# Two float32r score parts in 64-row tiles, in a two-layer transformer kernel

## The reference

```python
# layer 0: causal attention
qkv = x @ w_qkv
dots = einsum('bhid,bhjd->bhij', q, k) * d ** -0.5
dots = where(triu(ones, k=1), -inf, dots)
x = layernorm(x + (softmax(dots) @ v) @ w_out + b_out)
# ffn 0: ternary weights, silu(x @ wu) * (x @ wg) @ wd
# layer 1: 4 key/value heads shared by 16 query heads
q = (x * sigmoid(sum(abs(x)))) @ Wq;  k, v = split(x @ Wkv)
qk = q @ k.T / sqrt(16) - slope[h] * abs(i - j)
qk = where(abs(i - j) <= 32 or i < 64 or j < 64, -1e9, qk)
x = layernorm(x + (softmax(qk) @ v) @ Wo + bo)
# ffn 1: silu(x @ w_gate.T) * (x @ w_up.T) @ w_down.T
```

## Time and profile before

| what | us |
|---|---|
| median of 3 runs | 1196.45 (1194.09 to 1198.43) |
| the profiled execution | 1192.84 |
| its span, first to last instruction | 1191.1 |
| TensorE busy in the span | 1013.9 (85%) |
| VectorE busy | 734.6 (62%) |
| ScalarE busy | 576.1 (48%) |
| GpSimd busy | 323.0 (27%) |

### The profile page before, as it was taken

The page is one execution under the profiler, slowest core; times in us unless marked ns, Lnnn a source line. Parts: engine busy times, 40 slices in busy tenths (PEclk is TensorE's granted clock), DMA queues, the critical chain, the costliest instruction groups (busy, mean ns, idle before and its releaser), DMA issues. The chain is left out here.

```text
span 1191.1 us, 18123 instructions
## 1 busy us (share of the span) xinstructions
PE 1013.9 (85%) x6562; PEld 513.9 (43%) x6562; DVE 734.6 (62%) x1611; ACT 576.1 (48%) x1169; POOL 323.0 (27%) x391
## 2 busy tenths in 40 slices
PE   7924889989998899868468899999999998899996
PEld 4511232323333578654022333333333333588885
DVE  3653677777773556556457587777878773434422
ACT  3411466666665534316035476666767665423220
POOL 1040011111111345500433614224133240333332
PEclk9855899999999999969569799999999999999998
DMA  8585044333300000004952426254252100000001
GB/s 273 123 153 61 1 55 54 39 40 41 45 2 1 1 1 1 1 19 100 235 131 92 108 61 119 73 96 84 60 110 82 48 2 1 1 1 19 6 13 36
DMA packets 39636, 71.02 MB, mean 60 GB/s; under 512 B 7103, under 2 KB 23375, under 8 KB 38708
## 3 DMA queue, kind: packets, MB, share of 16 engines
q1 hardware_dynamic: 37660, 64.89, 26.8%
q0 software_dynamic: 1072, 3.80, 0.9%
q10 hardware_dynamic: 816, 1.18, 0.3%
HBM read 57.27 MB, written 12.32 MB: 58 GB/s over the span
## 5 line engine op out<-in xcount | busy, mean ns | idle before, releaser
L849 ACT ACTIVATE prob<-ps 128x512 f32<-128x512 f32 (+6 forms) x896 | 426.6, 539 | 341.3 <-PE ps L885 339.3
L885 PE MATMUL ps<-qop,kop 98*128 98x512 bf16 (+15 forms) x1376 | 285.3, 293 | 47.5 <-DMA qop<-mrow 29.0
L871 PE MATMUL ps<-kop,qop 96*128 96x512 bf16 (+4 forms) x896 | 265.3, 373 | 54.6 <-DVE maxes L790 27.9
L885 PEld LDWEIGHTS ps<-qop,kop 107*128 107x128 bf16 (+2 forms) x1376 | 108.2, 99 | 280.4 <-ACT prob L849 150.3
L912 PE MATMUL ps<-prob,vst 128*32 128x512 f32 (+4 forms) x1792 | 213.7, 549 | 5.2 <-POOL prob L739 5.2
L790 DVE CUSTOM_DVE_ANT_0 attn<-ps,alibi_table 128x960 bf16<-128x960 f32 x128 | 148.0, 1156 | 84.3 <-PE ps L871 67.8
L739 POOL TENSOR_TENSOR prob<-prob,keep 128x384 int32<-128x384 int32 (+2 forms) x144 | 121.2, 850 | 253.6 <-ACT prob L849 252.6
L790 DVE CUSTOM_DVE_ANT_0 tri<-ps,alibi_table 128x960 bf16<-128x960 f32 x128 | 147.8, 1155 | 24.1 <-PE ps L871 23.5
L1248 PE MATMUL ps<-xs,ffn_parts 128*128 128x512 f32 x640 | 150.5, 392 | 4.4 <-DVE hf L1222 2.3
L871 PEld LDWEIGHTS ps<-kop,qop 96*128 96x128 bf16 x896 | 77.7, 100 | 147.3 <-DVE maxes L790 82.7
L1248 PEld LDWEIGHTS ps<-xs,ffn_parts 128*128 128x128 f32 x640 | 119.0, 188 | 29.8 <-DVE hf L1222 3.1
(11 more groups left out here) (97 smaller groups left out, 722.2 us busy)
## 6 DMA issues: line engine op xcount, KB each, us to landing
alibi_table<-in_table SPq DMA_DIRECT2D x64, 336.0 KB, 4.3
qop<-q_parts SPq DMA_DIRECT2D x96, 128.0 KB, 7.1
kop<-k_parts SPq DMA_DIRECT2D x48, 128.0 KB, 7.8
kop<-k_parts SPq DMA_DIRECT2D x48, 96.0 KB
q_parts<-qop SPq DMA_DIRECT2D x8, 384.0 KB, 3.4
q_parts<-kop SPq DMA_DIRECT2D x8, 384.0 KB, 6.2
x<-in_x SPq DMA_DIRECT2D x4, 512.0 KB, 7.2
out<-x SPq DMA_DIRECT2D x4, 512.0 KB, 2.9
```

The costliest lines, as they stand in the source:

```text
L849: nc.scalar.activation(prob[0:rows, q % 2, k % HG, lo % CH:lo % CH + hi - lo], ps[0:rows, tile_bank(n, k), lo % CH:lo % CH + hi - lo], ACT ...
L871: last = nc.tensor.matmul(ps[:, slot + a // CH, a % CH:a % CH + b - a], qop[0:RD, par, qt // CT, h, i0 % CH:i0 % CH + P], kop[0:RD, par, h ...
L885: return nc.tensor.matmul(ps[0:rows, bank, a % CH:a % CH + b - a], lhs, rhs, start=start, stop=True, skip_group_check=True)
```

## The change

Scores are now made from two float32r parts (high: rounded to 12 bits of mantissa; low: the rest) in three products, high-high, high-low and low-high: 48 rows (`DOT`), with four position rows in layer 1 and two rows of maxima, 50 or 54 rows in all. Two heads of a pair stand in the two halves of the partitions, from row 0 and from row 64 (`ROW_TILE`), so that their matmuls address different 64-row tiles of the array. The units of a pair now alternate between the two heads. In `project` ScalarE writes the high part and VectorE the low one; the slots for parts are eight. The units of layer 0 come in another order, so that the parts of the first groups are ready first, and groups 0 and 1 are loaded within `project` in layer 0. The load of a group is 10 DMAs (12 in layer 1), some of 32 and some of 16 partitions, of float32. Layer 1 has two buffers (`L.bufs`) and loads group n + 1 at the third key tile of group n, held until the values of group n - 1 are done. The maxima are transposed in float32 and split after that. In `attend` the first rows of maxima are sent before the last group's load, and in layer 1 also before the second table. Position rows are rounded once at the start on GpSimd and written to DRAM. In layer 1 the last key tile of 64 keys is computed as a tile of 128, whose upper 64 lanes are used.

```diff
-RING = 4
+RING = 8
-PARTS = 3
-Q_PART = (0, 0, 0, 1, 1, 2)
-K_PART = (0, 1, 2, 0, 1, 0)
-BUFS = 3
+PARTS = 2
+HP = HG // 2
+ROW_TILE = P // 2
+DOT = 3 * HD
-NPOS = 9
+NPOS = 4
...
-        self.key_sets = HG if index == 0 else 3
+        self.key_sets = HP if index == 0 else 3
+        self.bufs = 3 if index == 0 else 2
...
-    return [(h, qt, *maximum_columns(layer, qt)) for half in range(2) for h in range(HG)
-            for qt in range(half * CT, (half + 1) * CT)]
+    return [(h, qt, *maximum_columns(layer, qt)) for half in range(2) for pair in range(HP)
+            for qt in range(half * CT, (half + 1) * CT) for h in (2 * pair, 2 * pair + 1)]
...
-            if q == 3 and BUFS <= n + 2 < N:
-                steps.append(("load", 0, n + 2))
+            if q == 3 - layer.index and n + layer.bufs - 1 < N:
+                steps.append(("load", 0, n + layer.bufs - 1))
...
+            for u in range(len(units)):
+                if u == first + 2:
+                    for k in range(first):
+                        sp.wait_ge(sent[k], stored(first, k))
                     operands.load(sp, 0)
+                elif u == first + 4 and L.bufs > 2:
+                    operands.load(sp, 1)
                 sp.wait_ge(part2, u + 1)
+                store(sp, u)
...
+                raw = K.staging
+                pool.dma_start(raw[0:QROWS, :], dram.qpos).then_inc(const_loaded, 16)
+                pool.dma_start(raw[QROWS:QROWS + KROWS, 0:T], dram.kpos).then_inc(const_loaded, 16)
...
+                nc.gpsimd.tensor_copy(rounded[0:QROWS, :], raw[0:QROWS, :]).then_inc(ones_set, 1)
...
-            def second_part(u):
-                r = rows_of(units[u][1])
-                act.wait_ge(rest1, u + 1)
-                nc.scalar.copy(part[u % RING][0:r, 1, :], rest[0:r, u % RING, :]).then_inc(part2, 1)
...
-            def third_part(u):
...
                 nc.vector.scalar_tensor_tensor(
-                    out=rest[0:r, u % RING, :], in0=ps[0:r, 2 + u % 4, :], scalar=0.25 if is_q(m) else 1.0,
-                    in1=part[u % RING][0:r, 0, :], op0=ALU.mult, op1=ALU.subtract).then_inc(rest1, 1)
+                    out=part[u % RING][0:r, 1, :], in0=ps[0:r, 2 + u % 4, :], scalar=0.25 if is_q(m) else 1.0,
+                    in1=part[u % RING][0:r, 0, :].bitcast(F32), op0=ALU.mult, op1=ALU.subtract).then_inc(part2, 1)
...
+        for a in range(2):
+            at = a * ROW_TILE
...
+            sp.dma_start(kop[at:at + 2 * HD, buf], key).then_inc(self.loaded[buf], 16)
+            sp.dma_start(kop[at + 2 * HD:at + DOT, buf], key[0:HD]).then_inc(self.loaded[buf], 16)
+            for e in range(2):
+                sp.dma_start(qop[at:at + 2 * HD, buf, e].rearrange("p h t -> p (h t)"),
+                             q_parts[0:1, e, n, a].to_broadcast((2, HD, HP * CH))).then_inc(self.loaded[buf], 16)
+            sp.dma_start(qop[at + 2 * HD:at + DOT, buf].rearrange("p e h t -> p e (h t)"),
+                         q_parts[1, :, n, a].rearrange("e d x -> d e x")).then_inc(self.loaded[buf], 16)
...
             if i == 1:
                 load_tables(0)
-                load_tables(1)
-            operands.load(sp, 1)
-            for k in range(RING):
-                sp.wait_ge(operands.sent[k], K.parts_in_dram[k])
-            operands.constants(sp, BUFS - 1)
-            operands.load(sp, BUFS - 1)
             for what, k, n in steps:
                 if what == "rows":
                     send_rows(n, k)
+                    if n == 0 and k == 0:
+                        if i == 1:
+                            load_tables(1)
+                        for slot in range(RING):
+                            sp.wait_ge(operands.sent[slot], K.parts_in_dram[slot])
+                        operands.constants(sp, L.bufs - 1)
+                        operands.load(sp, L.bufs - 1)
...
-                        nc.vector.tensor_copy(mrow[:, k, :], ps[:, ring_bank(what, k, n), :].bitcast(BF16)[:, 0:P]).then_inc(m_copied, 1)
+                        nc.vector.tensor_copy(mrow[:, k, 0, :], turned).then_inc(m_high, 1)
+                        dve.wait_ge(m_high, r + 1)
+                        nc.vector.tensor_tensor(mrow[:, k, 1, :], turned, mrow[:, k, 0, :].bitcast(F32),
+                                                ALU.subtract).then_inc(m_copied, 1)
...
-                i0 = qt * P
+                i0, at = qt * P, h % 2 * ROW_TILE
...
-                                            qop[0:RD, par, qt // CT, h, i0 % CH:i0 % CH + P],
-                                            kop[0:RD, par, h if i == 0 else 0, a:b], start=True, stop=True)
+                                            qop[at:at + RD, par, qt // CT, h // 2, i0 % CH:i0 % CH + P],
+                                            kop[at:at + RD, par, h // 2 if i == 0 else 0, a:b], start=True, stop=True)
...
-                        pe.wait_ge(m_cut, 2 * n + k + 1)
-                        nc.tensor.transpose(ps[:, ring_bank(what, k, n), :].bitcast(BF16)[:, 0:P],
-                                            mpart[:].rearrange("p k u -> p (k u)"), identb[:]).then_inc(m_turned, 1)
+                        pe.wait_ge(max_done, (2 * n + k + 1) * (NU // 2))
+                        nc.tensor.transpose(ps[0:NM, ring_bank(what, k, n), 0:P],
+                                            maxes[:, k].rearrange("p h t -> p (h t)"), ident[:]).then_inc(m_turned, 1)
```

288 lines of the change are left out of this document (138 added, 150 removed).

## The result

The changed kernel takes 1449.15 us (median of 6 runs, 1436.36 to 1466.12) against 1196.21 of the kernel before: ratio 1.2104, 95% interval 1.2068 to 1.2141. I had forecast 1180, faster. Its profiled execution, the fastest of the six, spans 1434.6 us against 1191.1, 243.5 more.

What follows compares the result with a forecast made beforehand. Attention takes most of the span, and TensorE never rests inside layer 1's key tiles. Terms -9 - 15 - 9 - 2 + 5 + 5 + 8.5 = -16.5 from 1192.84 give 1176.3, with 3.6 for the median 1180; range 1165 to 1195.

Steps and rivals of the forecast that it cites:

- step 3: Steady groups of layer 0: heads side by side -1.9 a group, weights and shape changes +0.8; -9 us in all.
- step 6: Steady groups of layer 1: side by side, weights and shape changes +5 us in sum, late operand loads +8.5.
- Steps 1 and 2: Layer 0's start: eight slots end the projection's slot wait, -9 us; first rows of maxima wait less behind loads, -15.
- the stores kept the rows of maxima waiting over 8 us: Sign of being wrong in kind, at layer 0's first rows of maxima, whose wait was taken as 3 us.
- Steps 4 and 5: Layer 1's start: 4, rows land sooner but second table as late as now, -2 us; 5, group 0's mask late, +5.
- Step 6 b: Layer 1's steady groups: float32 weight loads set the pace of short pieces, +2.5 us a group, between 0 and 6.1.
- Step 6 a: Layer 1's steady groups: tiles and units in different array halves overlap, -2.3 us a group, ends 0 and 9.
- Step 6 d: Layer 1, two buffers: operand load 1.4 us late in each of 6 groups against a 13.8 us window, +8.5.
- four-pass pieces: Rival: short float32r pieces take four passes, heads side by side; +16 us, 1196, 16%. The slower rival assumes them too.
- The loads at 122 GB/s: Rival: layer 1's operand loads run at 122 GB/s, 6 x 2.9 = +17 us, 1197, no change; 14%.
- The slower rival: Rival: short pieces take four passes and nothing runs side by side, in both layers' groups; 1252 us, 18%.

Runs made afterwards that it cites:

- e7: On top of e5, each score and exp matmul contracts 112 to 118 rows instead of 48 to 54, buffers filled ahead; 1239.48 us.
- e11: e2 with layer 1's tables, constants and operands ahead of its first rows of maxima again, as in the kernel before; 1331.73 us, ratio 1.1210 to before.
- e8: Kernel before, bf16 parts in 96 rows, with only the change's start of layer 0; 1172.88 us, ratio 0.9836.
- e2: On top of e1, parts of k stored by one transfer a unit over 128 (64) DRAM rows and loaded 16 rows at a time; 1353.26 us.
- e3: Kernel before, with first rows of maxima of each layer sent before loads of later operands and second tables; 1205.32 us, ratio 1.0093.
- e5: On top of e2, all four heads read the operands of rows 0 to 53, so one row tile; 1601.89 us.
- e1: Changed kernel, with each load repeating 16 rows of q twice replaced by loads of 16 rows each; 1369.56 us in one run.
- e4: Kernel before, with its bf16 score matmuls contracting 48 rows instead of 96, nothing else changed; 1286.60 us in one run.

## Why the prediction was wrong

It failed in what it took for granted, more than in its terms: above all in step 3 and step 6, whose groups were priced at a granted clock that the changed kernel doesn't get.

- **Granted clock: not a term at all.** I worked every duration at the clock of the rows before, in the one sentence of step 6 that I needed it and in all the others unsaid. The matmuls keep their columns, so I took them to keep their time. Rows 1 show the clock at 0.96 to 0.98 with 96 to 107 rows and no more can be read from them; that contraction over 48 rows in one tile need not keep it was not considered, and no rival had it. Set at full clock by e7, the steady groups cost 10.3 + 35.4 = 46 us more than before; in e11, whose transfers are the best that I tried together, they cost 57.3 + 78.3 = 136. The 90 us between are mostly the clock; late operands of layer 1 are in them too (28.9 us of idle time in e11, 11.1 of it before the groups), and what two tiles give back is taken off them.
- **Steps 1 and 2 (-24): right, then undone.** The mechanism is shown by e8 (first "exp" matmul at 82.02, forecast 81; 22.3 us at the end of the first group) and by e2 (78.51). In the changed kernel the first "exp" matmul stands at 115.06 instead of 105.32, so the same steps ended at +9.7, and the first group, at a granted clock of 0.52 instead of 0.79, adds 12.8 to make the 22.5 of the table. They ended there because I counted the stores by their bytes ("512 KB per unit instead of 384") and not by their form. I listed "the stores kept the rows of maxima waiting over 8 us" as a sign against me. They did worse: they kept the projection's slots, 7.63 and 4.84 us, and the block's end.
- **Step 3 (-9): wrong sign.** The groups stand 40.8 us apart, not 32.3. Of that 7.4 us, 1.5 is float32r at full clock (e7), where I had +0.8 for weights and shapes, and side by side takes 1.2 off again, where I had 1.9. The terms of the step were of the right kind; the rest, 7 us a group, is the clock.
- **Steps 4 and 5 (+3): mis-sized.** The first rows sent early in layer 1 cost 16.9 us in bf16 (e3) and 20.4 in float32r (e2 to e11). There are two chains. Step 4 had the second tables as late as the 9.3 us of before; VectorE waited 14.40 us for them in e3 and 16.14 in the changed kernel, and 31.24 instead of 16.28 for the first one behind the slow stores. The other is that of step 5, weights to GpSimd to the mask to TensorE (9.68 us in e3, 17.85 in the changed kernel), for which I took 18.8 us of slack from the earlier trace rows and reckoned the queue at the rate of an empty one. What I took as a gain of 5.7 us, rows that land sooner, was there (TensorE waits 3.17 us for them instead of 7.74), and was worth less than the queue behind it.
- **Step 6 b (+2.5 a group): the mechanism right, the size near its upper end.** At full clock the group costs 5.1 more (e7), against ends of 0 and 6.1. The records of the weight loads, 209 ns and more, don't refute the 129 that I took as their pace, as those of the feed-forward stage are as long at that pace. A part of the 5.1 is one that I put at nothing: the earlier trace rows gave 0.235 us for a float32r matmul of 512 columns, and I worked the long pieces as if they kept the 0.21 of the full clock. At 15 ns each for the hundred or so matmuls of 416 columns and more in a group, that is 1.6 us, an estimate. (The upper end by the skill's figure is 4.5, not 4.6; nothing hangs on it.) What it does was not quite what I said: ScalarE gets the first "exp" tile 0.18 us later, and the key tile is 3.29 us long against 2.88; that the chain of banks carries the delay on is my reading of it.
- **Step 6 a (-2.3 a group): right, and hidden by the clock.** Matmuls of two heads do start together: in the steady stretch of e2, 68 of 364 score and "exp" matmuls start within 20 ns of the one before, and none in e5. At the full clock that gives some 2.4 to 3.4 us a group in layer 1 against e7. The 249 us from e5 to e2 are another matter: they came with a clock of 0.70 instead of 0.51.
- **Step 6 d (+8.5): 64.6 us of idle time instead.** I gave a rate to the bytes "that go to 32 partitions" and asked how many partitions a transfer reaches. e1 moved the same bytes in as many transfers, to fewer partitions at a time, and the idle time fell to 8.7. The step that failed is the rate: 25.5 to 26.9 us for a load that I had at 12.8 to 18.1. The bytes were right, and the window of 13.8 us nearly so (14.7 in five of the six gaps, 18.2 in the first).
- **The rivals.** No four-pass pieces are to be seen: at the full clock the next matmul starts 28 ns after a piece of 32 columns in e7 and 29 ns after one in the kernel before (medians of 123 and 90), and e7 has no more than 5.1 us a group to account for, where four passes would have cost 8.2. The loads at 122 GB/s, whose rival had 18.1 us for one, are what e1 shows (17.1 to 18.1); those of the changed kernel are slower than any rival had them. The slower rival ended 56 us above before, for a reason that isn't there.

What is open: what the clock follows beside the rows, since e4 gets 0.50 and 0.89 with the same kind of matmuls; how the loss of the steady groups of layer 1 (111.1 us) splits between clock, loads and weights, as they interlock; why keys loaded 16 rows at a time are later than 32 (19.2 to 19.8 us for a group's load against 17.1 to 18.1; at the 118 GB/s of the earlier trace rows 1.97 MB are 16.7 us and 2 of landing, which fits the former but doesn't isolate it); and what the order of units alone does.

## What to carry to other kernels

Before halving the rows of a contraction, check that TensorE keeps its clock with the rows that are left: price the change once at the full and once at the half clock, and if TensorE bounds, run the old kernel with fewer rows first, an edit of two lines (e4) that gives the answer. Count a DMA by its outermost dimension, in DRAM above all, as well as by its bytes, and look at the DMA share while a queue is held up: a low share there meant few engines here, not much data. When a transfer is moved ahead of others, follow each of those to the engine that waits for it in order, and to what stands behind on that engine.
